# Attention and FFN layer on one core: probabilities turned through DRAM and VectorE blocks instead of TensorE, scores four tiles ahead, engine loops written out

## What is computed

```python
def layer(x):                                   # x: 16 x 1024 x 256
    n = layernorm(x)
    Q, K, V = n @ Wq.T + bq, n @ Wk.T + bk, n @ Wv.T + bv
    s = einsum('bqd,bkd->bqk', Q, K) / sqrt(256) * gaussian_mask(1024)
    x = x + (softmax(s) @ V) @ Wo.T + bo
    n = layernorm(x)
    h = gelu(n @ binarize(w1).T + b1)           # hidden size 1024, exact gelu
    return x + h @ binarize(w2).T + b2
```

## Time and profile before

| what | us |
|---|---|
| median of 3 executions | 1578.99 (1577.24 to 1581.0) |
| span of the profiled execution | 1576.1 |
| PE busy | 1553.5 (99%) |
| PE weight loads busy (beside the matmuls) | 1366.9 (87%) |
| VectorE busy | 1167.2 (74%) |
| ScalarE busy | 654.8 (42%) |
| GpSimd busy | 484.5 (31%) |

### The profile page before, as it was taken

How to read it: one execution, slowest core, us unless ns; L and a number is a source line. 1 busy time by engine, 2 the same in 40 slices (tenths; PEclk the granted TensorE clock), 3 DMA queues, 4 the chain that set the end, 5 groups by cost and what they waited for, 6 DMA issues and landing times.

```text
span 1576.1 us, 24294 instructions
## 1 busy us (share of the span) xinstructions
PE 1553.5 (99%) x9421; PEld 1366.9 (87%) x9421; DVE 1167.2 (74%) x2034; ACT 654.8 (42%) x838; POOL 484.5 (31%) x713
## 2 busy tenths in 40 slices
PE   8999999999999999999999999999999999999998
PEld 6888888898888888888888888889888888888887
DVE  8685867858678586885858768586785867858676
ACT  4452443624335253352533535334352443624333
POOL 4133151332413333132421423314133151333314
PEclk9999999999999999999999999999999999999999
DMA  4001001010000101001010010100101000010000
GB/s 154 1 1 54 1 15 42 1 54 1 29 28 1 54 1 55 1 1 54 1 56 1 3 52 1 56 1 14 41 1 56 1 21 34 1 54 1 28 1 27
DMA packets 10046, 39.31 MB, mean 25 GB/s; under 512 B 942, under 2 KB 3260, under 8 KB 7996
## 3 DMA queue, kind: packets, MB, share of 16 engines
q1 hardware_dynamic: 9888, 37.49, 6.2%
q10 hardware_dynamic: 28, 0.01, 0.0%
HBM read 20.72 MB, written 16.78 MB: 24 GB/s over the span
## 4 chain that ended last, share of the span: by engine, by line
PE 81%; DVE 14%; issue 2%; ACT 1%; DMA 1%; SPq 0%; POOL 0%; POOLq 0%; DVEq 0%
PE ps L712 20%; PE ps L733 15%; PE ps L735 8%; PE ps L722 7%; DVE gl L521 7%; PE ps L748 6%; PE ps L749 6%; PE ps L887 5%; DVE gh L519 5%; PE ps L690 2%; PE ps L699 2%; PE ps L700 2%; PE ps L702 2%; PE ps L687 2%; PE ps L688 2%; PE ps L757 2%
## 5 line engine op out<-in xcount | busy, mean ns | idle before, releaser
L372 ACT ACTIVATE pth<-ps 128x1024 fp32r<-128x1024 f32 x128 | 131.2, 1025 | 418.1 <-PE ps L722 418.1
L733 PE MATMUL ps<-vhl,pth 128*128 128x512 f32 x1024 | 268.7, 404 | 0.0
L748 PE MATMUL ps<-sgn,gh 128*128 128x256 f32 x1024 | 241.5, 281 | 0.9 <-DVE ys L528 0.4
L367 ACT ACTIVATE prob<-ps,nmax 128x1024 f32<-128x1024 f32 x128 | 142.1, 1111 | 233.8 <-PE ps L749 229.3
L749 PE MATMUL ps<-sgn,gl 128*128 128x256 f32 x1024 | 238.8, 279 | 0.0
L250 POOL TENSOR_TENSOR ve<-mv,eps 128x1 f32<-128x1 f32 x128 | 24.3, 190 | 669.3 <-DVE mv L505 669.3
L477 DVE TENSOR_REDUCE nmax<-ps 128x1 f32<-128x1024 f32 x128 | 156.6, 1224 | 92.7 <-PE ps L712 92.7
L733 PEld LDWEIGHTS ps<-vhl,pth 128*128 128x128 f32 x1024 | 182.9, 188 | 34.4
L482 DVE TENSOR_TENSOR ptl<-ps,pth 128x1024 fp32r<-128x1024 f32 x128 | 156.7, 1224 | 68.6 <-ACT pth L372 68.6
L748 PEld LDWEIGHTS ps<-sgn,gh 128*128 128x128 f32 x1024 | 192.9, 188 | 5.6 <-DVE ys L528 3.5
L749 PEld LDWEIGHTS ps<-sgn,gl 128*128 128x128 f32 x1024 | 192.9, 188 | 0.6
(11 more groups left out here) (112 smaller groups left out, 2774.9 us busy)
## 6 DMA issues: line engine op xcount, KB each, us to landing
out_dram<-xin SPq DMA_DIRECT2D x32, 512.0 KB, 2.6
xin<-in_L_attn_x_dram SPq DMA_DIRECT2D x15, 1024.0 KB, 4.9
xin<-in_L_attn_x_dram SPq DMA_DIRECT2D x2, 512.0 KB, 4.8
w1s<-in_L_ffn_w_dram SPq DMA_DIRECT2D x1, 1024.0 KB, 10.3
w2s<-in_L_ffn_w_dram SPq DMA_DIRECT2D x1, 1024.0 KB, 12.4
mask_bc<-mask_dram SPq DMA_DIRECT2D x1, 512.0 KB, 7.3
wk<-in_L_attn_Wk_dram SPq DMA_DIRECT2D x1, 256.0 KB, 5.5
wq<-in_L_attn_Wq_dram SPq DMA_DIRECT2D x1, 256.0 KB, 6.1
```

Of the source, the lines that this page charges most:

```text
L367: act.activation(two(prob[:, q % 2, :]), slot(q % 2), ACT.Exp, bias=nmax[:, q:q + 1], accum_out=rsum[:, q:q + 1]).then_inc(exp_set, 1)
L372: act.activation(two(pth[:, q % 2, :]), ps[:, PT_BANK:PT_BANK + 2, :], ACT.Copy).then_inc(pth_set, 1)
L733: pe.matmul(bank, pth[:, q % 2, tile(t)], vhl[:, t, :, :], start=t == 0, stop=False)
L748: pe.matmul(bank, gh[:, j, tile(t)], sgn2[:, j, :], start=j == 0, stop=False)
```

## The change

**The turn of the probabilities leaves PE.** ACT writes the exponentials of a tile in four blocks of 256 columns. SP stores the tile (512 KB) to a scratch tensor in DRAM, `p_wide`, waits for it, and loads it back so that each group of 32 partitions holds what belongs to it (`regroup_probs`). DVE then turns 32x32 blocks (`turn_probs`, one STREAM_TRANSPOSE of 128x1024, written with a step of 4 elements) into `pt` in SBUF. ACT copies the high part from `pt`, and POOL, not DVE, subtracts for the low part (`lo_probs`).

**Weighing the values** is 24 matmuls of 256 columns into one half bank; the second add of `add_attention` is gone.

**The order.** Four slots for the probabilities instead of two. Scores 1, 2 and 3 of the next batch run among the `ffn_rows` of this one, and each `weigh_values(q)` is followed by `scores(q + 4)`. `turn_rows`, `queries` and `values` are spread between the last `weigh_values`. The queue of SP carries the 8 round trips of a batch between the stores and loads, which now go by halves.

**Loops.** All batches are written out; there is no hardware loop.

```diff
 sync (SP):
+            def regroup_probs(b, q, first=False):
+                sp.wait_ge(exp_set, T * b + q + 1)
+                if not (first and q < 2):
+                    sp.wait_ge(p_back[q % 2], 16 * ((T // 2) * b + q // 2))
+                sp.dma_start(p_wide[q % 2].rearrange("(i p k) -> p i k", p=P, k=S // (P // QUAD)),
+                             prob[:, q % P_SLOTS, :].rearrange("p (i k) -> p i k", i=P // QUAD)).then_inc(p_out, 16)
+                sp.wait_ge(p_out, 16 * (T * b + q + 1))
+                sp.dma_start(prob[:, q % P_SLOTS, :],
+                             p_wide[q % 2].rearrange("(p k) -> p k", p=P)).then_inc(p_back[q % 2], 16)
+            def batch(b, s, more, load_more):
+                for q in range(TH, T):
+                    regroup_probs(b, q)
...
+                store(b, s, first, 1)
+                if load_more:
+                    load(b, s, first)
+                store(b, s, 1 - first, 2)
+                if load_more:
+                    load(b, s, 1 - first)
+                if more:
+                    regroup_probs(b + 1, TH - 1)
 gpsimd (POOL):
+            def lo_probs(b, q):
+                pool.wait_ge(pth_set, T * b + q + 1)
+                pool.tensor_tensor(ptl[:, q % P_SLOTS, :], pt[:, q % P_SLOTS, :],
+                                   pth[:, q % P_SLOTS, :].bitcast(F32), ALU.subtract).then_inc(ptl_set, 1)
 vector (DVE):
-            def lo_probs(b, q):
-                dve.wait_ge(pth_set, T * b + q + 1)
-                dve.tensor_tensor(two(ptl[:, q % 2, :]), ps[:, PT_BANK:PT_BANK + 2, :],
-                                  two(pth[:, q % 2, :].bitcast(F32)), ALU.subtract).then_inc(ptl_set, 1)
+            def turn_probs(b, q):
+                dve.wait_ge(p_back[q % 2], 16 * ((T // 2) * b + q // 2 + 1))
+                dve.transpose(pt[:, q % P_SLOTS, :].rearrange("p (j c g) -> p g j c", j=T, c=QUAD),
+                              prob[:, q % P_SLOTS, :].rearrange("p (g j r) -> p g j r", j=T, r=QUAD)).then_inc(pt_set, 1)
+            def head(b, rows_of):
+                row_max(b, 0)
+                row_max(b, 1)
+                if rows_of is not None:
+                    scale_outputs(rows_of, range(0, 3))
+                turn_probs(b, 0)
+                row_max(b, 2)
+                if rows_of is not None:
+                    scale_outputs(rows_of, range(3, 5))
+                turn_probs(b, 1)
+                if rows_of is not None:
+                    scale_outputs(rows_of, range(5, T))
+                turn_probs(b, 2)
+                row_max(b, 3)
 tensor (PE):
-                bank = ps[:, OUT_BANK + q % 2, :]
-                for t in range(T):
-                    pe.matmul(bank, pth[:, q % 2, tile(t)], vhl[:, t, :, :], start=t == 0, stop=False)
-                for t in range(T):
-                    last = pe.matmul(bank[:, 0:D], ptl[:, q % 2, tile(t)], vh[:, t, :], start=False, stop=t == T - 1)
+                bank = ps[:, OUT_BANK + q % 2, 0:D]
+                for j in range(T):
+                    pe.matmul(bank, pth[:, q % P_SLOTS, tile(j)], vh[:, j, :], start=j == 0, stop=False)
+                    pe.matmul(bank, pth[:, q % P_SLOTS, tile(j)], vl[:, j, :], start=False, stop=False)
+                    last = pe.matmul(bank, ptl[:, q % P_SLOTS, tile(j)], vh[:, j, :], start=False, stop=j == T - 1)
...
+            def batch(b, s, more):
+                for q in range(4):
                     weigh_values(b, q)
+                    scores(b, q + 4)
...
+                weigh_values(b, 4)
+                turn_rows(b + 1, 0)
+                weigh_values(b, 5)
+                turn_rows(b + 1, 1)
+                queries(b + 1, range(0, 2))
+                weigh_values(b, 6)
+                queries(b + 1, range(2, QG))
+                weigh_values(b, 7)
...
+                scores(b + 1, 1)
+                ffn_rows(b, range(0, 3), True)
+                scores(b + 1, 2)
+                ffn_rows(b, range(3, T), True)
+                scores(b + 1, 3)
+                pe.wait_ge(ffn_scaled, T * (b + 1))
```

More of the change, by code:

```diff
@@ new lines, in batch @@
+            def batch(b, s, more, load_more):
+                for q in range(TH, T):
+                    regroup_probs(b, q)
+                if more:
+                    for q in range(TH - 1):
+                        regroup_probs(b + 1, q)
+                first = 1 if more else 0
+                store(b, s, first, 1)
[6 more added lines that the diff above has]
+                    regroup_probs(b + 1, TH - 1)
@@ L231, in _ @@
+            for q in range(TH):
+                regroup_probs(0, q, True)
+            for b in range(B):
+                batch(b, b % 2, b < B - 1, b < B - 2)
+            for n in range(N2):
+                sp.wait_ge(y_stored[n], 16 * B)
         @block.gpsimd
@@ L425, in batch @@
                 load_table(b, ACT.Exp)
-            with act.Fori(0, PAIRS - 1) as i:
-                batch(i, 0, True)
-                batch(i, 1, True)
-            batch(PAIRS - 1, 0, True)
-            batch(PAIRS - 1, 1, False)
+                head(b + 1)
+            head(0)
+            for b in range(B):
+                batch(b, b % 2, b < B - 1)
         @block.vector
@@ L551, in _ @@
+            for n in range(N2):
+                dve.wait_ge(x_loaded[0][n], 16)
+                stats_attention(0, range(n * TH, (n + 1) * TH))
             dve.wait_ge(stats1, T)
@@ new lines, in _, with batch @@
+            head(0, None)
+            def batch(b, s, more):
+                r, loads = 1 - s, (b + 1) // 2 + 1
+                invert_sum(0)
+                add_attention(b, s, 0)
+                if more:
+                    dve.wait_ge(x_loaded[r][1], 16 * loads)
+                    stats_attention(r, range(TH, T))
+                row_max(b, 4)
+                add_attention(b, s, 1)
+                turn_probs(b, 3)
+                normalize_ffn(b, s, 0)
+                row_max(b, 5)
+                if more:
+                    dve.wait_ge(x_loaded[r][0], 16 * loads)
+                    stats_attention(r, range(TH))
+                add_attention(b, s, 2)
+                turn_probs(b, 4)
+                normalize_ffn(b, s, 1)
+                if more:
+                    dve.wait_ge(stats1, T * (b + 2))
+                row_max(b, 6)
+                if more:
+                    aggregate_attention(b + 1)
+                add_attention(b, s, 3)
+                turn_probs(b, 5)
+                normalize_ffn(b, s, 2)
+                row_max(b, 7)
@@ L673, in turn_rows, with queries @@
                 last.then_inc(x_turned, 1)
-            def queries(b, first):
-                for k in range(QG):
+            def queries(b, groups, first=False):
+                for k in groups:
                     n, m = divmod(k, C)
@@ new lines, in weigh_values, with ffn_rows @@
+                for j in range(T):
+                    pe.matmul(bank, pth[:, q % P_SLOTS, tile(j)], vh[:, j, :], start=j == 0, stop=False)
+                    pe.matmul(bank, pth[:, q % P_SLOTS, tile(j)], vl[:, j, :], start=False, stop=False)
+                    last = pe.matmul(bank, ptl[:, q % P_SLOTS, tile(j)], vh[:, j, :], start=False, stop=j == T - 1)
+                last.then_inc(pv_summed, 1)
+            def ffn_rows(b, rows_now, more):
+                for r in rows_now:
+                    t = row_tile(r) if more else r
+                    if r < 2 and more:
+                        pe.wait_ge(vl_set, VG * (b + 1) + 3 + r)
+                    elif r < 2:
+                        pe.wait_ge(x1_set, T * b + T - 1 + r)
+                    else:
+                        pe.wait_ge(ffn_scaled, T * b + r - 1)
+                    if not more and r % TH == 0:
+                        pe.wait_ge(gl_set, J * b + (J // 2) * (r // TH + 1))
+                    bank = ps[:, OUT_BANK + r % 2, 0:D]
+                    for j in range(J):
+                        if more and r == 0:
+                            pe.wait_ge(gl_set, J * b + j + 1)
+                        pe.matmul(bank, gh[:, t, j, :], sgn2[:, j, :], start=j == 0, stop=False)
+                        last = pe.matmul(bank, gl[:, t, j, :], sgn2[:, j, :], start=False, stop=j == J - 1)
@@ L822, in _ @@
             pe.wait_ge(ml_set, 1)
-            queries(0, True)
+            queries(0, range(QG), True)
             pe.wait_ge(diag_set, C)
@@ L828, in _ @@
             last.then_inc(alpha2_spread, 1)
-            values(0)
+            values(0, range(VG), True)
             for k in range(2 * C):
@@ L875, in batch @@
                     turn_rows_ffn(b, n, 2 * n)
[L876 removed]
+                    values(b + 1, range(2 * n, 2 * n + 2))
                 for j in range(J):
```

484 lines of the change are left out of this document (245 added, 239 removed).

## The result

The changed kernel takes 1708.74 us (median, 1702.51 to 1709.74), the kernel before 1578.34 beside it: ratio 1.0815, 95% interval 1.0802 to 1.0829. It is 8% slower; I had forecast 5% faster.

What follows compares the result with a forecast made beforehand. PE's own work was taken as the bound. From 1576.1 us: 15 batches at -5.1 (76.5), loop -8.6, first tiles +7, last batch -3, giving 1495.0; plus 2.9, 1498 us. Forecast range 1478 to 1530; 8 in 10, 1455 to 1576.

Steps and rivals of the forecast that it cites:

- The sign that I had set: Mark of a wrong forecast: weigh_values on PE waiting for ptl in every batch, the path being longer than thought.
- Part 1: PE's own work: turn and weighing save 0.92 us a tile, 7.4 a batch; the loop's stops save 8.6 in all.
- The weighing: PE's weigh_values: 24 matmuls of 256 columns take about 2.73 us a tile against 2.86, 0.13 less.
- The loop stops: PE's seven waits for issue at the ends of hardware loop passes go: 8.6 us saved.
- Part 2, the transpose: DVE's turn of a tile's probabilities takes 1.2 us, upper bound 2.4 if the strided write costs as much again.
- rival 1: DVE's transpose takes about 2.4 us because of its strided write: 75 us more, 1573 in all; chance 0.18.
- The rule that I set beside it: SBUF has 16-byte lines and charges accesses crossing to a new one, so DVE's transpose write could cost more; not priced.
- Part 2, the low part on POOL: POOL's subtraction takes 2.4 us a tile, 19.5 a batch, bringing POOL to 49 us; not the bound.
- Part 3, the trip of tile 3: DRAM round trip of 6.1 us, about 3 us of x traffic ahead; hidden up to 7.3, so costed at nothing.
- rival 2: The DRAM round trip is too long: each us above 7.3 costs 2 a batch; 1583 us and more; chance 0.15.
- Part 3, VectorE's list at the end of the tiles: After weigh_values(4), DVE needs 11.9 us before the first ql, PE 9.8: PE waits 2.3 us a batch.
- 1.2 us of slack: Between weigh_values(q) and weigh_values(q+4), PE works 19.2 us and the tile's path takes 18, so it fits.

Runs made afterwards that it cites:

- the run with the short subtraction: The changed kernel with POOL subtracting the low part for only 128 of a tile's 1024 columns: 1635.10 us, ratio 1.0348.
- the run with all three costs out: The changed kernel with unit-stride transposes, no round trip and POOL's low part for 128 of 1024 columns: 1492.09 us, ratio 0.9450.

## Why the prediction was wrong

The sign that I had set came true: weigh_values waits for ptl in every batch. The sums of the prediction come out, but for two slips that change nothing: the bound of the round trip is 11.1 us, not 10.7 (2 x 5.2 + 2 x 0.35), and 8 x 2.4 is 19.2.

- **Part 1** was right in the turn. The weighing was mis-sized: 2.83 us a tile in the run with all three costs out (776.63 to 779.46), not 2.73; that is 0.8 a batch. I took the 0.113 of the earlier trace rows, which is another loop of matmuls. The loop stops were worth 13 us, not 8.6.
- **Part 2, the transpose: the step that failed first.** I took 1.2 by the earlier trace rows; it is 2.02. All those rows are of unit or plain strides, and the cost lies in the write's step. My rival 1 had the mechanism at a chance of 0.18, and a price of 75 us for 1.2 us more; 0.79 more cost 65. The rule that I set beside it, 16-byte lines in "SBUF — State Buffer" of the Trainium skill, agrees with the runs: 1.23 us with unit stride and 2.02 with a step of 16 bytes. Steps between the two were not run.
- **Part 2, the low part on POOL: a cost that I did not see.** Its 2.4 us was right. That VectorE's xn is held off meanwhile stood nowhere in the sum; it is worth 37 us or more, and with the subtraction's length in the path 74. In the kernel before no xn starts beside POOL's long subtraction, and all take 0.40 to 0.42 us. But the earlier trace rows had the sign: the cast L519 has a mean of 885 ns, and its median is 687. One a batch takes 2.1 to 2.4 us, shown above at the run with the short subtraction; I read the mean as the price of a cast, and as the lower bound of a transpose. The Trainium skill says it: "SBUF — State Buffer", section "Who interferes with whom", has the shared ports taken by whichever of a VectorE operation in a 2-port mode and a GpSimd one comes first, for the whole instruction, and names tensor_scalar. The runs agree that it is held for the whole instruction (0.66 us in the mean with the long subtraction, 0.48 in pieces, 0.39 without); in which mode xn runs none of them shows.
- **Part 3, the trip of tile 3: seen, costed at nothing, and the largest miss.** The text has "about 3 us in front of tile 3" and "the cover is gone at 7.3", and does not put the two together. From the store's issue (790.92) to the turn (800.19) it is 9.3 us. Without the trip 100 us are gone, with one leg 61, with another order on the queue 8 at most; how much of a leg's length is due to x beside it was not tested. The time lies in the range of rival 2 (1583 and more), but by more than its mechanism: it priced a trip that is long for every tile. In the batch shown three of the eight stores took 4.9 to 5.4 us (tiles 3 and 4, and tile 1 of the next batch), the others 2.9 to 3.2, and at weigh_values PE waited for tile 3 alone.
- **Part 3, VectorE's list at the end of the tiles: right.** Forecast 2.3 us a batch for ql; with the three costs out it is 21.0/17 = 1.2, and the batch 91.02 against 90.9. That these two are so near is in part luck: 0.8 more for the weighing and 1.1 less for this wait nearly cancel.
- **The clock** I left at full. Behind the waits for ptl and ql it is at 0.6 for 4.4 us; net it costs 24 us.
- **Combination.** I priced the rivals one at a time. A longer transpose, a longer trip and a held-off VectorE sit on one path with 1.2 us of slack. Singly they are worth 65, 100 and 74 us, together 217, a little less than their sum, and far outside a range in which the others stood at their forecast.

## What to carry to other kernels

When work moves from a full engine to idle ones, the sum of busy times says little: price the longest path of one tile with its slack, and ask which queue carries the tile that is behind other traffic. A slack of 1.2 us in a path of 18 is no cover for five estimated prices. Time each new operation in the access pattern that it will have, and look at what a long GpSimd instruction in SBUF does to its neighbour on VectorE (a row whose mean lies well above its median is a sign of it); several short ones in its place took 20% more time on GpSimd and gave back 2% of the kernel.

## What the hardware showed that I had not expected

- A 128x1024 fp32 transpose in 32x32 blocks on VectorE takes 1.23 us with blocks written at unit stride and 2.02 us at a step of 16 bytes.
- Beside GpSimd's work in SBUF the tensor_scalar xn, the cast gh and, five times in the kernel before, the subtraction gl (1.65 us instead of 1.23) on VectorE took longer. In the changed kernel an xn begun just behind the start of the 2.4 us subtraction takes 2.44 to 2.49 us in each batch instead of 0.40; transposes (2.0 us), bn_stats (0.41) and the adds of PSUM to the rows (0.48) begun beside it take as long as elsewhere.
- Four stores of 128 KB in pieces of 1 KB took 7.7 to 9.2 us with an outermost dimension of 4; loads of the same pieces landed after 2.6 us each with one of 32.
- SBUF to SBUF, 512 KB in four transfers landed after 3.5 us, about one leg of the way through DRAM (2.9 out, 3.4 back).
- Matmuls of 256 columns start 0.113 us apart in the FFN rows and 0.118 in the weighing; I did not find out why.
